# Four normalising multiplications of local attention probabilities as one product of two tensors

## The reference

```python
sim = jnp.einsum('bhwid,bhwjd->bhwij', bq, bk)      # i: 128 queries, j: 256 keys
mask = (i < j) | (i > j + WINDOW) | (j == -1)
sim = jnp.where(mask, -jnp.finfo(sim.dtype).max, sim)
attn = jax.nn.softmax(sim, axis=-1)
out = jnp.einsum('bhwij,bhwjd->bhwid', attn, bv)
```

## Time and profile before

| | |
|---|---|
| median of 3 runs | 3022.46 us (3020.24 to 3024.24) |
| span of the profiled execution, first to last instruction | 3020.0 us |
| TensorE busy | 2762.9 us, 91% |
| VectorE busy | 2486.9 us, 82% |
| ScalarE busy | 1772.8 us, 59% |
| GpSimd busy | 1344.8 us, 45% |
| mean granted TensorE clock | 0.985 of full speed |

### The profile page before, as it was taken

The page is one execution under the profiler, slowest core; times in us unless marked ns, Lnnn a source line. Parts: engine busy times, 40 slices in busy tenths (PEclk is TensorE's granted clock), DMA queues, the critical chain, the costliest instruction groups (busy, mean ns, idle before and its releaser), DMA issues.

```text
span 3020.0 us, 63211 instructions
## 1 busy us (share of the span) xinstructions
PE 2762.9 (91%) x21580; PEld 1915.3 (63%) x21580; DVE 2486.9 (82%) x7195; ACT 1772.8 (59%) x4149; POOL 1344.8 (45%) x949
## 2 busy tenths in 40 slices
PE   2399998999999999999989999899999999999998
PEld 2167675676656676666766667567665667666675
DVE  3489897888879887898878988788887988889795
ACT  2147673567636776376744767357663677637674
POOL 1145443545335454355534544344543545434542
PEclk9799999999999999999999999999999999999999
DMA  5100001000000000000010000100000000000000
GB/s 155 34 2 6 7 8 32 3 6 4 24 18 5 5 7 24 15 5 5 8 30 9 6 4 8 36 3 5 5 22 20 5 5 7 24 15 5 5 8 18
DMA packets 57885, 46.22 MB, mean 15 GB/s; under 512 B 18438, under 2 KB 54876, under 8 KB 57444
## 3 DMA queue, kind: packets, MB, share of 16 engines
q1 hardware_dynamic: 53520, 35.14, 4.2%
q10 hardware_dynamic: 4052, 7.04, 0.7%
HBM read 25.33 MB, written 8.44 MB: 11 GB/s over the span
## 4 chain that ended last, share of the span: by engine, by line
PE 67%; DVE 12%; ACT 5%; POOL 4%; issue 4%; DMA 4%; DVEq 0%; ACTq 0%; POOLq 0%
PE ps L134 13%; PE ps L135 12%; PE ps L136 11%; PE ps L399 7%; PE ps L425 7%; PE ps L410 5%; DMA XS<-xu 4%; PE ps L334 3%; PE ps L385 3%; PE ps L353 2%; PE ps L293 2%; DVE ar_b L787 1%; ACT ar_b L562 1%; DVE ar_b L771 1%; POOL small L889 1%
## 5 line engine op out<-in xcount | busy, mean ns | idle before, releaser
L889 POOL TENSOR_TENSOR small<-small,neg_half 128x16 f32<-128x16 f32 x128 | 406.2, 3174 | 432.5 <-DVE small L734 430.7
L562 ACT ACTIVATE ar_b<-ar_b,small 128x256 f32<-128x256 f32 (+1 forms) x1024 | 492.9, 484 | 113.9 <-DVE small L771 111.5
L771 DVE CUSTOM_DVE_ANT_0 ar_b<-ps,mask_t,small 128x256 f32<-128x256 f32 (+1 forms) x1024 | 419.3, 462 | 36.2 <-PE ps L399 35.5
L893 POOL TENSOR_TENSOR ar_c<-ar_c 128x1024 f32<-128x1024 f32 x128 | 301.7, 2357 | 227.5 <-DVE ar_c L760 227.0
L787 DVE TENSOR_SCALAR ar_b<-ar_b,rsw 128x256 f32<-128x256 f32 (+1 forms) x1024 | 304.4, 360 | 9.1
L241 POOL TENSOR_SCALAR stats<-stats 128x2 f32<-128x2 f32 x128 | 29.9, 234 | 598.0 <-DVE stats L819 253.2
L134 PE MATMUL ps<-wqkv_hi,ht_hi 128*128 128x512 f16 x768 | 292.5, 381 | 0.0
L136 PE MATMUL ps<-wqkv_hi,ht_lo 128*128 128x512 f16 x768 | 291.6, 380 | 0.0
L135 PE MATMUL ps<-wqkv_lo,ht_hi 128*128 128x512 f16 x768 | 291.5, 380 | 0.0
L399 PE MATMUL ps<-ar_a 64*128 64x128 f32 x3840 | 270.5, 282 | 14.2 <-ACT ar_a L552 14.2
L410 PE MATMUL ps<-id_f,ar_b 128*128 128x128 f32 x1920 | 268.7, 275 | 9.6 <-DVE ar_b L787 9.2
(11 more groups left out here) (171 smaller groups left out, 6689.8 us busy)
## 6 DMA issues: line engine op xcount, KB each, us to landing
xu<-in_L_attn_x_dram SPq DMA_DIRECT2D x32, 256.0 KB, 2.9
out_dram<-xu SPq DMA_DIRECT2D x64, 128.0 KB, 2.9
XS<-xu SPq DMA_DIRECT2D x128, 63.5 KB
ar_a<-in_L_ffn_wqkv_dram ACTq DMA_DIRECT2D x1, 3072.0 KB, 17.2
modb<-mod_rows SPq DMA_DIRECT2D x8, 384.0 KB, 5.5
XS<-xu SPq DMA_DIRECT2D x112, 0.5 KB
ar_a<-in_L_wmod_dram SPq DMA_DIRECT2D x1, 1536.0 KB, 9.1
xu<-in_L_ffn_w_dram SPq DMA_DIRECT2D x1, 1364.0 KB, 9.7
```

The source lines that it names most:

```text
L562: last = act.activation(pw, pw, ACT.Exp, bias=mnw[:, n % 2, h:h + 1], scale=-1.0, accum_out=smw[:, n % 2, h:h + 1])
L771: last = dve.tensor_tensor_reduce(out=PW[:, f, q, i, c:2 * P], in0=ps[:, bk, i * 256 + c:(i + 1) * 256], in1=mask_t[:, c:2 * P], scale=rin ...
L889: pool.tensor_tensor(rinv[:, n % 4, :], ssm[:, n % 2, :], neg_half[:, 0:16], ALU.pow).then_inc(s_rinv, 1)
L893: pool.tensor_tensor(M1[:, n % 2, :], M1[:, n % 2, :], M2, ALU.add).then_inc(s_add, 1)
```

## The change

The four `tensor_scalar` operations of an `nm` piece, each with one head's inverse sum as a scalar for each partition, become one `tensor_tensor` over all four heads. Its second operand is the tensor of the four inverse sums, spread along the keys with a step of zero. So that the four inverse sums lie in the order of `q` and `i`, in which `PW` has the heads, ScalarE writes its row sums to column `4f + 2q + i` of `smw`, in place of `4f + q + 2i`.

```diff
                         for i in range(2):
-                            h = 4 * f + q + 2 * i
+                            h, k2 = 4 * f + q + 2 * i, 4 * f + 2 * q + i
                             pw = PW[:, f, q, i, c:2 * P]
                             last = act.activation(pw, pw, ACT.Exp, bias=mnw[:, n % 2, h:h + 1], scale=-1.0,
-                                                  accum_out=smw[:, n % 2, h:h + 1])
+                                                  accum_out=smw[:, n % 2, k2:k2 + 1])
...
                         dve.reciprocal(rsw[:, n % 2, 4 * f:4 * f + 4], smw[:, n % 2, 4 * f:4 * f + 4]).then_inc(s_rsw, 1)
                         dve.wait_ge(s_rsw, at(*piece))
                         c = 0 if n % NT else P
-                        for q in range(2):
-                            for i in range(2):
-                                h = 4 * f + q + 2 * i
-                                pw = PW[:, f, q, i, c:2 * P]
-                                last = dve.tensor_scalar(pw, pw, rsw[:, n % 2, h:h + 1], None, ALU.mult)
-                        last.then_inc(s_pn, 1)
+                        pw = PW[:, f, :, :, c:2 * P].rearrange("p q i k -> p (q i) k")
+                        inv = rsw[:, n % 2, 4 * f:4 * f + 4].unsqueeze(2).broadcast_to((P, 4, 2 * P - c))
+                        dve.tensor_tensor(pw, pw, inv, ALU.mult).then_inc(s_pn, 1)
```

## The result

The change made the kernel slightly slower: 3026.09 us in the median of 20 runs (3021.01 to 3031.64), beside 3021.26 us for the kernel before (20 runs, 3013.08 to 3024.28). The ratio is 1.0016, with a 95% interval from 1.0009 to 1.0022. The forecast was 3027.5 us and "the same within 0.2%". With one idle time of TensorE filled, the change costs 7.6 us, and the experiments put the missing 3 us down to TensorE's clock, which fell less often in these runs. Neither number was in the forecast.

A forecast was written before the change was run, and what follows sets the result against it. TensorE was taken to set most of the time, VectorE in places. 2.6 us for longer pieces on the chain plus 2.4 for GpSimd's wait made 5.0 us on 3022.5, so 3027.5 us, range 3017 to 3034.

The forecast's parts named there:

- What bounds it, and 37 pieces on the chain: TensorE sets most of the time, VectorE in places; about 37 of 256 `nm` pieces lie on the chain, 42 us.
- 0.07 us for each full piece: One product of 1.21 us replaces four operations of 1.14; over 37 chain pieces 2.6 us more.
- rival of a dearer product: The product takes 1.32 us, L752's mean: 6.7 us on the chain, 3031.6 us in all; chance 0.12.
- GpSimd at the fifth window: Piece at 620.12: L243 waits about 0.8 us for the product; 0.3 us arrives in each of 8 sequences, 2.4 us.
- in full: GpSimd's wait at 620.12 costs 0.8 us in each sequence, 6.4 us, time 3031.5; chance 0.18.
- The two pieces of 2.00 us, and the short ones, for nothing: Pieces at 590.90 and 711.80 give VectorE 13 us, 32 short ones 6 us; both counted as nothing for the total.
- faster: VectorE's 0.8 us at 590.90 and 711.80 reaches TensorE: 6.4 us gain if half, 12.8 if all, time 3014.7; chance 0.12.
- VectorE's busy time: Falls by about 4 us: 16 more for full pieces, 6 less for short ones, 14 less for GpSimd meetings.
- both dear cases: GpSimd's full wait and the dearer product together, given as the range's upper end, 3034 us.
- half of the faster case: Half of VectorE's saving at 590.90 and 711.80 reaching TensorE, given as the range's lower end, 3017 us.

The follow-up runs named there:

- f2: Changed kernel with 14 unread matmuls filling TensorE's wait, but four operations in the fifth window's piece that meets GpSimd: 3015.03 us, 0.9978 of the kernel before.
- g1: Kernel before with the wait filled, the one product only in the first piece of the fifth window: 3014.93 us, 0.9982 of the kernel before.
- g3: Changed kernel with the wait filled, the product in the fifth window's first piece cut into two halves: 3017.74 us, 0.9991 of the kernel before.
- f3: Kernel before with the wait filled, the one product only in the short pieces and the two of 2.0 us: 3011.28 us, 0.9963 of the kernel before.
- f0: Kernel before with 14 unread matmuls filling TensorE's wait for the last normalised pair of the second layer: 3012.7 us, 0.9969 of the kernel before.
- g0: The filled kernel before, same text, run again as base of the third group: 3011.33 us, 0.9971 of the kernel before.
- first group: Follow-up runs without the filled wait, on where in the kernel the price is paid; the kernel before beside them took 3020.9 us.

## Why the prediction was right, and where it was off

The total was right, at 4.8 us for 5.0. It was right in part by luck: with the wait filled the change costs 7.6 us, and the clock hid some of that.

- **What bounds it, and 37 pieces on the chain.** Right. L785 has 1.5% of the chain after, some 45 us, or 37 pieces of 1.225. They are in each sequence the first full one, the second half of the fifth window in place of its first, and the last ones. The 37 is a quotient of times: the chain touches 49 pieces, some only in part.
- **0.07 us for each full piece.** The product took 1.225 us, not 1.21, so it is 0.085, and 37 of them 3.1 us in place of 2.6. `f2`, which has the product everywhere but at the fifth window, measured 2.3 by the medians and 2.8 by its trace. L752 at 1.22 us was the right row: the step of zero in the innermost dimension costs nothing that shows, so the rival of a dearer product fell. The row of the errata's table that the prediction took from the Trainium skill, "VectorE: DVE Perf Modes", gives too little for the product (1.13 against 1.225) and far too little for the four operations (0.78 against 1.14). The same section of the Trainium skill says of this row that it "under-predicts single-op duration", and its formula for a float32 `tensor_tensor`, (N+151)/0.96, gives 1.224 and 0.691 us for the two forms; the trace agrees (1.225 and 0.69). The half price for each element of a `tensor_scalar` shows in the trace (0.52 against 1.04 ns), and what the row has too small is the fixed part.
- **GpSimd at the fifth window.** This is the term that was mis-sized: 2.4 us predicted, 3.6 (medians) to 4.2 or 4.6 (trace) measured in `g1`. The mechanism was right and its first step wrong. I let L241 through and made L243 wait for 0.8 us. It is L241 that waits, from its start to the end of the product, 1.07 us, and L825 is 1.04 us late instead of 0.8. Half of it gets through to the end of the sequence, 0.53 to 0.58 of 1.04, where I took 0.3 of 0.8. The rival "in full" was too dear. My reason, the gaps between four operations, told half of it. `g3` shows a gap letting L241 in (0.76 us), and so do the two sequences of before in which it took 0.38 us. But in the earlier trace rows, as in six of the eight, it needed no gap: its 0.22 us (from 620.13) lay inside the first `tensor_scalar`, which the other three follow from 620.42, some 0.03 us later than usual. In the seven traces that have four operations at this place, L241 was held to 0.38 us in 6 of 56 sequences. The rule of the Trainium skill, "SBUF — State Buffer", section "Who interferes with whom", names an operation with two inputs in SBUF, and it would have given the full wait for L241. The trace agrees with it here, at 1.29 against 0.22 us. The same section of the Trainium skill names `tensor_scalar` too, where it runs in its faster mode, and says that whoever issues first keeps the other out; the six waits of 0.38 us agree with that.
- **The two pieces of 2.00 us, and the short ones, for nothing.** Right. Each product there ends in 1.22 us, GpSimd waits instead (0.76 and 0.68 us), and `f3`, which has just these, isn't measurably faster than `f0` and `g0`. The rival "faster" fell with it.
- **VectorE's busy time.** I said 4 us less, and it was 6.8 more. The `nm` pieces themselves are at plus 0.4 (304.4 and 304.9 us on the two pages): the groups' busy time of before counts 276.4 us for the full ones, and after 282.3, less 5.5 for the short ones. The prediction's terms give nearly that with 0.085 for 0.07 (19 less 5.5 and 14 us). The rest is on L760: 105.6 us in place of 97.9 for one of its forms. Of its 128 operations, 24 take over 0.9 us in place of 16. In each sequence one more is held for 1.65 us in place of 0.68, by GpSimd's L905, which began 0.60 us before it; in before, the two L760 at this place took 1.28 us together and GpSimd's product waited (2.13 us).
- **The range and a remainder.** The ends of the range don't follow from the sums: both dear cases give 3022.5 + 6.7 + 6.4 = 3035.6 us, not 3034, and half of the faster case gives 3021.1 or, without the 5.0 us, 3016.1, not 3017. Of the product L243 would have met 0.90 us, not 0.93. Neither changes the forecast.
- **What was not in it: the clock.** I took the distance of 2.5 us between span and median for what lies around an execution, where each run lies 1.7 to 1.8 us above its own span, and the 4 us between the three runs for noise. Much of the latter is how often TensorE's clock falls behind an idle time that the change doesn't touch. In the 20 runs of after the mean granted clock was 0.987, and in the 27 of before in the first group 0.985. At half speed for the difference, that is 2 x 0.002 x 3020 = 12 us less at 1.2 GHz, or three to four stretches of 3.4 us by 1.1 us: some 4 us. This is the order of the 3 us between 7.6 and 4.8. Why the clock fell less often after the change isn't shown. The low stretch doesn't begin at a fixed point of the program: between sequences it begins 15.7 to 17.2 us behind the last reciprocal in the trace of before, 15.9 to 18.1 in that of after. So a change of 1 us in the length of a sequence can move it, but this was only argued.

## What to carry to other kernels

Ahead of replacing several VectorE operations with a scalar operand by one with two tensors in SBUF, look in the timeline for the GpSimd operations that start within it, however short: here all three waited until the product had ended, and what counts is who waits for them. Fewer instructions are no gain by themselves: here four took less time than one, because each element cost half.

Where a change moves the time by less than 1%, compare the granted clock of the executions ahead of the medians, and compare runs of equal clock. Measure the part that was changed between two fixed instructions of the trace, or take the scatter away first (here by filling one idle time of TensorE). That alone gained 0.3%, more than the change cost.

## What the runs showed of the hardware

- Behind the same idle time of TensorE of 2.69 us, the granted clock stays at 2.4 GHz, or falls to 1.2 GHz for 3.4 or 6.8 us, in different sequences of one execution. The 3.4 us cost 1.1 us. With 14 matmuls of 384 columns in the idle time (2.45 us), it didn't fall at this place between sequences in any of the eight filled traces. Behind the last sequence, where no next one follows, it still fell in seven of the eight.
- A VectorE product with two inputs in SBUF holds up a GpSimd operation of 0.22 us that starts 12 ns after it for 1.07 us, until about its end. Beside four `tensor_scalar` of 256 elements the same operation, started as soon behind the first, took 0.22 us in 50 of 56 sequences and 0.38 us in six.
- For each element a float32 `tensor_scalar` in SBUF took 0.52 ns (starts 0.196 us apart with 128 elements, 0.263 with 256), and a `tensor_tensor` 1.04 ns (0.691 us for 512, 1.225 for 1024).
- GpSimd's product L896, begun 0.33 us into a VectorE product, waits (1.80 against 1.04 us), and begun 0.55 us into four `tensor_scalar` it made these wait instead (2.00 against 1.14).
- The inverse sums spread with a step of zero along the innermost dimension cost no more than an ordinary second operand: 1.225 us against 1.22 for L752 of the same size.
